# Setup in the order of tile 0, and products of constants in five waits of TensorE

## The chip, the cores and the metric

The kernel runs on one core of a Trainium2 chip. A core has TensorE (PE: matmuls and transposes, results in PSUM), VectorE (DVE), ScalarE (ACT), GpSimd (POOL) and SyncE (SP, which issues most DMAs). Each engine executes its own instructions in the order in which they are written; they wait for one another by semaphores. The metric is the device time of one launch in microseconds (us).

## The reference

Four transformer-like layers run in a row over `x` of 64 sequences x 64 tokens x 256 channels, all modulated by a condition vector per sequence:

```python
# L0: modulated layernorm, attention of 16 heads x 16, projection, second modulated layernorm
gamma = w @ Wg.T + bg;  beta = w @ Wb.T + bb
h   = gamma * (layernorm(x) * ln_g + ln_b) + beta
qkv = h @ Wqkv.T + bqkv
h1  = softmax(q k^T) / 16 @ v @ Wp.T + bp + x
x   = gamma * (layernorm(h1) * ln_g + ln_b) + beta + h1
# L1: attention of 16 heads x 64 with normalised q and k; then 8 experts, each takes its top 512 of 4096 tokens
shift = silu(t) @ W_ada.T + b_ada
h   = layernorm(x) * g + b + shift
...
tok = tok.at[idx].add(gate * (gelu(ln(tok[idx]) @ fc1 + b1) @ fc2 + b2))
# L2: modulated attention of 16 heads x 64, feed-forward 256 -> 1024 -> 256 with gelu
# L3: RMS norm, attention of 16 heads x 16 with rotary positions, gated feed-forward
```

Everything is float32.

## The kernel before, in words

The 4096 tokens stand as 32 tiles of 128 tokens (two sequences each) and 256 channels; `x` stays in SBUF. The program of each engine is written out by hand, layer by layer: setup, L0 (`pe_narrow`, `dve_narrow`, `act_narrow`, `pool_narrow`), L1 (`pe_attention`, ...), routing, the eight experts (`pe_ff` with `Q["moe"]`), L2, its feed-forward, L3, its feed-forward. No scheduler moves anything: the order on an engine is the order of the code, and `after`/`wait_ge` are the semaphore waits.

**Setup.** SP loads the constants, the columns and the condition (`ld["small"]`), then four tiles of `x` (`x0`), the modulation weights of L0 and L1 (`m0`, `m1`), the next four tiles (`x1`), the L0 weights (`ld["l0"]`, two loads) and the rest. DVE measures mean and variance of tiles 0 to 7 and takes their inverse roots by three Newton steps (`dve_first_block`, twelve small instructions; the thirteenth, `dve_shift`, gives `shift`), then prepares many constants for later layers (`dve_setup`), and last turns the modulation products that PE left in `psS` into the tables `g0`, `b0`, `g1`, `b1`. `su["table"]` tells that they are there; `following(eng, "setup")` is the wait for it. PE multiplies the condition by `m0` and `m1` (`pe_setup`), waits for the tables, and transposes `g0` and `b0` into rows, which ACT copies out (`rows0`, sent to DRAM for L1).

**Tile 0 of L0.** ACT normalises tile n (`normalise`: `x * rstd + shift`), PE transposes it (`turn_x`), ACT applies the tables (`modulate`), PE makes q and k (`qk`), ACT adds the bias (`biased`), PE makes v (`values`), ACT copies it; `bias_product` goes between. PE runs `turn_x(0)`, `qk(0)`, `turn_x(1)`, `values(0)`, `bias_product`, `qk(1)`, `turn_x(2)`, `values(1)`, and then the loop over tiles begins with `scores(0)`.

**The later places.** In L1 and L2 the last tile (31) has no next tile whose projections could fill PE's wait for the softmax. Before the first expert's products PE waits for the normalised tokens after `turn(0, 0)` and `turn(0, 1)`. Before L2, all outputs of the experts are added in DRAM (`moe_sum`), and the first tiles are loaded back before DVE can normalise them; PE's first instruction there is `pe_transpose_x(pe, L, 0)`.

In the trace one float32 matmul of the program is two records (x8 is four matmuls), and so is a load of weights.

Of the kernel before, what the change touches and what calls it, by code (L numbers as in the profile page):

```python
# [128 lines left out]
def build_program(nc, A, out):  # L129
    ctx = ExitStack()  # L130
    with ctx:
# [196 lines left out]

        def pe_transpose_x(pe, L, n):
# [149 lines left out]
        def pe_attention(pe, L):  # L479
# [6 lines left out]
            def first():  # L486
                pe_transpose_x(pe, L, 0)
# [7 lines left out]
            def step(t, ahead, behind):  # L495
# [12 lines left out]
                else:  # L508
                    finish_before()
                    if L.li == 2:  # L510
                        after(pe, L.s["v"], NT)
                        for k in range(KC):
                            pe_ff_turn(pe, Q["l2"], 0, k)
                pe_transpose_probs(pe, L, t)
# [153 lines left out]
        def pe_narrow(pe, L):  # L668
# [10 lines left out]
            else:  # L679
                pe.wait_ge(L.ready, 16 * L.loads)  # L680
                turn_x(0, 0)
                qk(0)
                turn_x(1, 0)
                values(0, 2)
# [3 lines left out]
                values(1, 3)  # L688
            pe.wait_ge(su["bias"], 1 if L.li == 0 else 2)
# [85 lines left out]
        def dve_first_block(v, ch):  # L775

            for i in range(2):
                v.wait_ge(ld[f"x{i}"], 16)
                dve_group_moments(ch, i)
            dve_rsqrt(ch, rstd[:, 0:8], moments[:, 0:8, 1])  # L780
            dve_shift(0, 8)
# [402 lines left out]
        def act_narrow(a, L):  # L1184
# [15 lines left out]
            def normalise(n):  # L1200

                a.wait_ge(su["shift"], max(1, n // 4))
# [22 lines left out]
            if L.li == 0:  # L1225
                normalise(0)
                normalise(1)
            modulate(0, 0)
# [3 lines left out]
            biased(0)  # L1232
            if L.li == 0:
# [325 lines left out]
        def pe_ff(pe, Q):  # L1559
# [732 lines left out]
        def pe_setup(pe):  # L2292

            pe.wait_ge(ld["small"], 48)
            pe.wait_ge(ld["first"], 16)
# [5 lines left out]
            pe.wait_ge(su["table"], 1)  # L2301
# [5 lines left out]
            pe.wait_ge(su["rows"], 1)  # L2307
# [30 lines left out]
        def act_setup(a):  # L2338
            a.wait_ge(ld["small"], 48)
            nc.scalar.activation(silT, condT, ACT.Silu).then_inc(su["silu"], 1)  # L2340
            a.wait_ge(su["turned_rows"], 1)
# [13 lines left out]

        def dve_setup(v, ch):
            v.wait_ge(ld["small"], 48)
            ch.reset()
# [4 lines left out]
            ch.link(nc.vector.tensor_scalar(c("l0_bv", 0, 2), c("l0_bv", 0, 2), 1.0 / 16, None, ALU.mult))  # L2363
            ch.link(nc.vector.tensor_copy(table("g1"), over_batches(c("l1_g", 0, 2))))
            ch.link(nc.vector.tensor_reduce(head_mask[:, 0:8], ident.rearrange("p (a s) -> p a s", s=16), AX.X, ALU.add))
# [543 lines left out]
```

## Time and profile before

| | before |
|---|---|
| device time, median of 3 runs | 2655.84 us (2652.8 to 2656.27) |
| the profiled execution's own time | 2656.11 us |
| its span, first to last instruction | 2654.3 us |
| PE busy | 2477.9 us, 93% of the span |
| DVE busy | 1775.8 us, 67% |
| ACT busy | 1208.9 us, 46% |
| POOL busy | 509.4 us, 19% |
| chain of work that ended last | PE 79%, DMA 7%, DVE 7%, issue 2%, ACT 2%, POOL 2% |
| mean granted TensorE clock | 0.971 |

Times in all rows are microseconds from the span's start unless marked ns. The granted clock is 1.00 at 2.4 GHz and 0.50 at 1.2 GHz. L572 is line 572 of the kernel before. A row's "idle before" in square brackets is how long its engine had sat idle, and what ended that. DVE busy 67% is an average: in the first 42 us PE waits for chains of small instructions, and later it is nearly always busy.

### The profile page before, as it was taken

What the parts mean: (1) busy time and instruction counts of PE and PEld (TensorE: products, weight loads), DVE (VectorE), ACT (ScalarE), POOL (GpSimd) and SP (SyncE); (2) the same over time, 40 slices, a digit from 0 to 9 for tenths busy, and PEclk for the clock granted to TensorE, in tenths of its full rate; (3) what the DMA queues carried; (4) which work ended last, traced back from release to release, by engine and by line L of the source; (5) the groups of instructions that cost most, each with busy time, mean ns of one, the idle gap of its engine ahead of it and who ended that gap; (6) DMA issues with size and microseconds to landing.
All of it is one profiled execution on the core that took longest, in us unless ns stands there. A gap on an engine that the chain in (4) does not pass through costs nothing.

```text
span 2654.3 us, 64384 instructions
## 1 busy us (share of the span) xinstructions
PE 2477.9 (93%) x25825; PEld 1938.8 (73%) x25825; DVE 1775.8 (67%) x3968; ACT 1208.9 (46%) x2524; POOL 509.4 (19%) x488
## 2 busy tenths in 40 slices
PE   6999699999999965999899999999999899989999
PEld 5887366666666644888788888887766677779998
DVE  4888688788887766554445545545555499877676
ACT  4887365556555621343233333333343577633333
POOL 1323010001000104554111011011001256600000
PEclk9999899999999966999899999999999999999999
DMA  6000000000000032453300000000000133300000
GB/s 219 3 3 2 20 25 24 24 32 24 24 24 32 16 105 62 132 142 64 130 0 0 0 0 0 0 0 1 1 1 0 34 115 112 103 9 9 17 17 17
DMA packets 72165, 102.28 MB, mean 39 GB/s; under 512 B 10880, under 2 KB 50304, under 8 KB 71488
## 3 DMA queue, kind: packets, MB, share of 16 engines
q1 hardware_dynamic: 65856, 91.46, 10.7%
q0 software_dynamic: 6144, 8.56, 1.7%
q8 instruction: 111, 1.82, 0.3%
q14 instruction: 54, 0.44, 0.1%
HBM read 67.20 MB, written 32.80 MB: 38 GB/s over the span
## 4 chain that ended last, share of the span: by engine, by line
PE 79%; DMA 7%; DVE 7%; issue 2%; ACT 2%; POOL 2%; SPq 1%; DVEq 0%; ACTq 0%; POOLq 0%
PE psW L349 17%; PE psW L342 9%; PE psP L1569 8%; DMA rotated<-work 6%; PE psP L461 4%; PE psS L1758 4%; PE psP L468 4%; PE psS L1768 4%; PE psO L1569 4%; PE psO L441 3%; PE psS L408 3%; PE psW L572 3%; PE psO L373 2%; PE psP L424 2%; PE psW L1569 2%
## 5 line engine op out<-in xcount | busy, mean ns | idle before, releaser
L349 PE MATMUL psW<-r,work 128*128 128x512 f32 x1024 | 481.7, 604 | 1.0 <-DVE work L866 1.0
L1393 POOL TENSOR_TENSOR work<-work 128x512 f32<-128x512 f32 x128 | 132.0, 1042 | 1133.7 <-DVE work L900 1133.6
L349 PEld LDWEIGHTS psW<-r,work 128*128 128x128 f32 x1024 | 180.7, 191 | 162.4 <-issue 156.8
L342 PE MATMUL psW<-work,r 128*128 128x128 f32 x2048 | 245.3, 279 | 1.3 <-DVE work L866 1.0
L342 PEld LDWEIGHTS psW<-work,r 128*128 128x128 f32 x2048 | 236.4, 194 | 4.2 <-DVE work L866 1.4
L1301 ACT ACTIVATE work<-work 128x512 f32<-128x512 f32 x128 | 80.1, 625 | 278.0 <-DVE work L879 278.0
L864 DVE TENSOR_TENSOR work<-psW,tab 128x256 f32<-128x256 f32 x64 | 27.0, 422 | 185.0 <-PE psW L335 185.0
L572 PE MATMUL psW<-work,r 128*128 128x128 f32 x1024 | 132.8, 283 | 8.0 <-ACT work L1194 5.7
L2106 ACT ACTIVATE work<-psP 128x512 f32<-128x512 f32 x64 | 38.2, 597 | 214.6 <-PE psP L1569 214.6
L572 PEld LDWEIGHTS psW<-work,r 128*128 128x128 f32 x1024 | 121.1, 194 | 16.0 <-ACT work L1194 6.6
L1569 PE MATMUL psP<-r 128*128 128x256 f32 x512 | 127.0, 386 | 5.0 <-DVE r L1845 3.0
L468 PEld LDWEIGHTS psP<-work,r 128*128 128x128 f32 x992 | 118.0, 192 | 14.8 <-issue 7.4
L461 PE MATMUL psP<-r,work 128*128 128x256 f32 x512 | 127.5, 383 | 1.2 <-ACT work L1317 1.2
L1174 ACT ACTIVATE work<-psO,col 128x512 f32<-128x512 f32 x128 | 92.5, 773 | 75.7 <-PE psO L373 75.6
L1317 ACT ACTIVATE work<-psO 128x512 f32<-128x512 f32 x128 | 69.5, 595 | 118.1 <-PE psO L441 118.1
L468 PE MATMUL psP<-work,r 128*128 128x128 f32 x992 | 120.7, 275 | 0.0
L1250 ACT ACTIVATE work<-work 128x512 f32<-128x512 f32 x128 | 80.6, 630 | 80.9 <-DVE work L890 78.6
L922 DVE RECIPROCAL work<-psO 128x256 f32<-128x256 f32 x64 | 112.1, 1751 | 0.9 <-PE psO L556 0.9
L1758 PE MATMUL psS<-work,r 128*128 128x512 f32 x256 | 111.5, 593 | 0.3 <-ACT work L2149 0.3
L1569 PEld LDWEIGHTS psP<-r 128*128 128x128 f32 x512 | 97.5, 193 | 19.4 <-DVE r L1845 3.4
L461 PEld LDWEIGHTS psP<-r,work 128*128 128x128 f32 x512 | 93.4, 192 | 24.9 <-ACT work L1317 8.8
L877 DVE TENSOR_REDUCE work<-psS 128x8 f32<-128x512 f32 x128 | 87.8, 686 | 33.5 <-PE psS L408 33.5
(353 smaller groups left out, 5495.8 us busy)
## 6 DMA issues: line engine op xcount, KB each, us to landing
r<-in_l_fc SPq DMA_DIRECT2D x16, 1024.0 KB
rotated<-work SPq DMA_DIRECT2D x60, 256.0 KB
work<-mod_rows SPq DMA_DIRECT2D x64, 128.0 KB, 2.9
work<-rotated SPq DMA_DIRECT2D x30, 256.0 KB
r<-in_l_w SPq DMA_DIRECT2D x2, 3072.0 KB, 14.6
x<-in_x SPq DMA_DIRECT2D x8, 512.0 KB, 9.3
gather_table<-work SPq DMA_DIRECT2D x32, 128.0 KB, 1.8
moe_sum<-work SPq DMA_DIRECT2D x32, 128.0 KB, 1.7
```

The costliest lines, as they stand in the source:

```text
L342: ins = nc.tensor.matmul(ps[:, q * P:(q + 1) * P], w[:, k, lo + q * P:lo + (q + 1) * P], L.hT[:, k, :], start=(k == 0), stop=(k == KC - 1))
L349: ins = nc.tensor.matmul(ps[:, 0:width], L.hT[:, k, :], w[:, k, lo:lo + width], start=(k == 0), stop=(k == KC - 1))
L461: ins = nc.tensor.matmul(psP[:, 0:D], L.oT[:, j, :], l1_wout[:, j, :], start=(j == 0), stop=(j == FJ - 1))
L468: ins = nc.tensor.matmul(out_bank(L, t)[:, q * P:(q + 1) * P], l2_wout[:, j, q * P:(q + 1) * P], L.oT[:, j, :], start=(j == 0), stop=(j == ...
L572: ins = nc.tensor.matmul(psW1[:, q * P:(q + 1) * P], w[:, k, q * P:(q + 1) * P], L.hT[n % L.far][:, k, :], start=(k == 0), stop=(k == KC - 1))
L877: ch.link(nc.vector.tensor_reduce(mx, ps, AX.X, ALU.max))
L922: ch.link(nc.vector.reciprocal(L.rec, psO[:, 256:512].rearrange("p (k n) -> p k n", n=P)))
L1174: nc.scalar.activation(L.qk[:, 4 * i:4 * i + 4, :], ps, ACT.Identity, bias=c("l1_qn", g + 1), scale=c("l1_qn", g)).then_inc(L.s[f"e{i}"].s ...
L1393: nc.gpsimd.tensor_tensor(E, E, halves(L.rs)[i].unsqueeze(2).broadcast_to([P, 8, N]), ALU.mult).then_inc(L.s[f"prob{i}"].sem, 1)
L1569: ins = nc.tensor.matmul(bank[:, 256 * i:256 * i + 256], w[:, at:at + P], h, start=first and i == 0, stop=i == 1, skip_group_check=True)
L1758: ins = nc.tensor.matmul(psS[:, q * 512:(q + 1) * 512], Q.w2[u][:, j, q * P:(q + 1) * P], Q.hid[:, j, :], start=(n == 0), stop=(n == FJ - 1))
L1768: ins = nc.tensor.matmul(ps, Q.hid[:, j, r * P:(r + 1) * P], Q.w2[u][:, j, :], start=(n == 0), stop=(n == FJ - 1))
```

## The change

Three things are changed.

1. **DVE's setup is in another order.** The first block of four tiles (moments, roots, shift) comes first, then the modulation tables `g0` and `b0` (and with them `su["table"]`), then the second block of four, and only then the constants and `b1`. There are now two root blocks of four columns where there was one of eight. `normalise(n)` waits for its own block.
2. **PE and ACT don't wait for the whole setup before tile 0.** `normalise(0)` and `turn_x(0)` no longer wait for the tables; the weights are waited for after `turn_x(0)`. The transposes of `g0` and `b0` and ACT's copy of them are now inside tile 0 (`pe_mod_rows`, `act_mod_rows`), behind `su["mask4"]`. The load of `l0_w` goes ahead of that of `x1`.
3. **`pe_keep_busy(bank, times)`** multiplies the identity by 256 columns of constants into a PSUM bank that nobody reads, in five places: 5 times while the first loads are under way, 5 in the last tile of L1, 4 before the first expert, 10 and 6 before L2 (the 6 behind a wait for the first rows loaded back), 6 in the last tile of L2.

```diff
+        def pe_keep_busy(bank, times):
+            for _ in range(times):
+                nc.tensor.matmul(bank[:, 0:256], ident, consts[:, 0:256], start=True, stop=True)
 # pe_attention, first():
+                if L.li == 2:
+                    pe_keep_busy(psS, 10)
+                    pe.wait_ge(ld["first"], 32)
+                    pe_keep_busy(psS, 6)
                 pe_transpose_x(pe, L, 0)
 # pe_attention, step(), last tile only:
+                    pe_keep_busy(psO, 6 if L.li == 2 else 5)
                 pe_transpose_probs(pe, L, t)
 # pe_narrow, L0:
+                turn_x(0, 0)
                 pe.wait_ge(L.ready, 16 * L.loads)
-                turn_x(0, 0)
                 qk(0)
                 turn_x(1, 0)
+                pe_mod_rows(pe)
                 values(0, 2)
 ...
                 values(1, 3)
+                pe.wait_ge(su["rows"], 1)
 # DVE
-        def dve_first_block(v, ch):
-            for i in range(2):
-                v.wait_ge(ld[f"x{i}"], 16)
-                dve_group_moments(ch, i)
-            dve_rsqrt(ch, rstd[:, 0:8], moments[:, 0:8, 1])
-            dve_shift(0, 8)
+        def dve_first_block(v, ch, i):
+            lo, hi = 4 * i, 4 * i + 4
+            v.wait_ge(ld[f"x{i}"], 16)
+            dve_group_moments(ch, i)
+            dve_rsqrt(ch, rstd[:, lo:hi], moments[:, lo:hi, 1])
+            dve_shift(lo, hi)
 ...
-            dve_first_block(v, ch)
+            dve_first_block(v, ch, 0)
+            dve_modulation(v, ch)
+            dve_first_block(v, ch, 1)
             dve_setup(v, ch)
 # act_narrow
-                a.wait_ge(su["shift"], max(1, n // 4))
+                a.wait_ge(su["shift"], n // 4 + 1)
 ...
                 normalise(1)
+                a.wait_ge(su["table"], 1)
             modulate(0, 0)
             modulate(1, 0)
             normalise(2)
             biased(0)
+                act_mod_rows(a)
 # pe_ff
                 turn(0, 1)
+                pe_keep_busy(psS, 4)
 # pe_setup
             pe.wait_ge(ld["small"], 48)
+            pe_keep_busy(psW0, 5)
             pe.wait_ge(ld["first"], 16)
 ...
-            pe.wait_ge(su["table"], 1)
+        def pe_mod_rows(pe):
+            pe.wait_ge(su["mask4"], 1)
             for i, name in enumerate(("g0", "b0")):
 ...
-            pe.wait_ge(su["rows"], 1)
 # SP
+            sp.dma_start(l0_w, chunked("l0_w")).then_inc(ld["l0"], 16)
             load_x(1)
-            sp.dma_start(l0_w, chunked("l0_w")).then_inc(ld["l0"], 16)
```

DVE at the start, before: the roots of eight tiles, then (rows left out here are constants) the tables last. `newton` is the scratch of the roots, `cond` and `tab` hold modulation and tables.

```order
L739 SCALAR_TENSOR_TENSOR rstd<-newton 128x8
L785 SCALAR_TENSOR_TENSOR shift<-moments,rstd 128x8
L63 ISA
L2363 TENSOR_SCALAR col<-col 128x2
L2364 COPY tab<-col 128x128
L2365 TENSOR_REDUCE head_mask<-consts 128x8
...
L2380 TENSOR_TENSOR head_mask<-head_mask 128x4
L2361 TENSOR_TENSOR cond<-psS,col 128x256
L2361 TENSOR_TENSOR tab<-cond,col 128x128
L2361 TENSOR_TENSOR cond<-cond,col 128x128
```

And now, from the end of the first root block on:

```order
L751 SCALAR_TENSOR_TENSOR rstd<-newton 128x4
L797 SCALAR_TENSOR_TENSOR shift<-moments,rstd 128x4
L2380 TENSOR_TENSOR cond<-psS,col 128x256
L2380 TENSOR_TENSOR tab<-cond,col 128x128
L2380 TENSOR_TENSOR cond<-cond,col 128x128
L2387 TENSOR_TENSOR tab<-cond 128x128
L763 BN_STATS stat<-x 128x6 x4
L766 BN_AGGR mv<-stat 128x2 x4
L768 COPY moments<-mv 128x8
```

The four table instructions stand behind the first shift; the second block and all constants moved behind them.

PE at the start, before. L2288 is the modulation, L2305 the transposes of the tables, L335 `turn_x`, L572 `qk`, L594 `values`:

```order
L2288 MATMUL psS<-cond,r 128x64 x12
L2305 MATMUL psS<-consts,tab 64x128 x4
L335 MATMUL psW<-consts,work 128x128 x2
L572 MATMUL psW<-work,r 128x128 x8
L335 MATMUL psW<-consts,work 128x128 x2
L594 MATMUL psW<-r,work 64x128 x8
```

And now (L332 are the products of constants, L2324 the transposes of the tables):

```order
L332 MATMUL psW<-consts 128x256 x5
L2304 MATMUL psS<-cond,r 128x64 x12
L340 MATMUL psW<-consts,work 128x128 x2
L582 MATMUL psW<-work,r 128x128 x8
L340 MATMUL psW<-consts,work 128x128 x2
L2324 MATMUL psS<-consts,tab 64x128 x4
L604 MATMUL psW<-r,work 64x128 x8
```

The transposes of the tables moved from ahead of `turn_x(0)` to behind `turn_x(1)`, and five products of constants stand ahead of everything.

PE from the last expert to L2's first q and k, before:

```order
L1768 MATMUL psS<-r,work 128x256 x16
L1768 MATMUL psP<-r,work 128x256 x16
L335 MATMUL psW<-consts,work 128x128 x2
L342 MATMUL psW<-work,r 128x128 x32
L349 MATMUL psW<-r,work 128x512 x4
```

And now:

```order
L1783 MATMUL psS<-r,work 128x256 x16
L1783 MATMUL psP<-r,work 128x256 x16
L332 MATMUL psS<-consts 128x256 x16
L340 MATMUL psW<-consts,work 128x128 x2
L347 MATMUL psW<-work,r 128x128 x32
```

Sixteen products now stand between the experts and the first transpose (L340), which waits for `xn`; the eleventh of them waits for `ld["first"]`.

## Rows read from the trace of the kernel before

**Rows 1.** Chain that ended last, 0 to 60 us: start, us, what

```profile
41.59 0.25 PE psP L607 x2
```

**Rows 2.** Timeline, 0 to 45 us: start, us, engine, line, idle before

```profile
7.58 1.41 DVE L751 BATCH_NORM_STATS2 stat<-x 128x6 f32<-128x256 f32 x4 [7.58 <-DMA x<-in_x]
...
9.10 5.35 PE L2288 MATMUL psS<-cond,r 128*128 128x64 f32 x24 [9.10 <-DMA r<-in_l_mod]
...
11.26 1.41 DVE L751 BATCH_NORM_STATS2 stat<-x 128x6 f32<-128x256 f32 x4 [1.66 <-DMA x<-in_x]
...
13.32 0.17 DVE L733 TENSOR_SCALAR newton<-moments 128x8 f32<-128x8 f32 x1
...
15.76 0.17 DVE L785 SCALAR_TENSOR_TENSOR shift<-moments,rstd 128x8 f32<-128x8 f32 x1
...
19.64 0.42 DVE L2361 TENSOR_TENSOR cond<-psS,col 128x256 f32<-128x256 f32 x1
...
21.75 1.06 PE L2305 MATMUL psS<-consts,tab 128*64 128x128 f32 x4 [7.29 <-DVE tab L2389]
22.85 0.59 ACT L2342 ACTIVATE work<-psS 64x512 f32<-64x512 f32 x1 [17.99 <-PE psS L2305]
...
25.34 1.27 ACT L1194 ACTIVATE work<-psW,tab 128x64 f32<-128x64 f32 x4
```

**Rows 3.** DMA issues, 0 to 50 us: KB each, us to landing

```profile
r<-in_l_w SPq DMA_DIRECT2D x1, 768.0 KB, 8.2
...
r<-in_l_wp SPq DMA_DIRECT2D x1, 256.0 KB, 8.4
```

**Rows 4.** Windows of L572: stretch, its us, PE busy, PEld busy, PEclk, DMA, GB/s

```profile
26.00:30.50 4.50, 3.79 (x16) 3.49 (x16) 1.00 1.04 403
42.00:44.30 2.30, 2.05 (x16) 1.86 (x16) 1.00 0.08 9
```

**Rows 5.** Windows: PE, PEld, DVE, ACT, POOL busy, then PEclk

```profile
944.00:954.00 10.00, 6.50 (x78) 5.54 (x79) 2.10 (x6) 2.28 (x4) 2.01 (x2) 0.50 0.01 2
...
1033.00:1043.00 10.00, 6.53 (x17) 4.99 (x17) 6.73 (x9) 1.19 (x2) 7.83 (x6) 0.50 0.21 56
```

**Rows 6.** Timeline at the end of L1, last tile

```profile
942.72 0.61 PE L476 MATMUL psP<-r,work 128*128 128x8 f32 x4 [2.06 <-ACT work L1287]
...
946.29 1.97 PE L424 MATMUL psP<-consts,work 128*128 128x128 f32 x8 [2.96 <-DVE gates L1032]
...
951.39 5.11 PE L461 MATMUL psP<-r,work 128*128 128x256 f32 x16 [1.21 <-ACT work L1317]
```

**Rows 7.** Timeline at the first expert

```profile
1031.88 1.97 PE L1555 MATMUL psW<-consts,work 128*128 128x128 f32 x8
...
1037.31 3.78 PE L1569 MATMUL psP<-work,r 128*128 128x256 f32 x8 [3.47 <-DVE work L1845]
...
1046.24 1.89 PE L1569 MATMUL psP<-work,x 128*128 128x256 f32 x8
```

**Rows 8.** Timeline at the start of L2

```profile
1266.74 0.75 DVE L761 BATCH_NORM_STATS2 stat<-x 128x6 f32<-128x256 f32 x2 [6.78 <-DMA x<-moe_sum]
...
1270.75 0.66 PE L335 MATMUL psW<-consts,work 128*128 128x128 f32 x2 [11.64 <-DVE work L850]
...
1272.38 10.31 PE L342 MATMUL psW<-work,r 128*128 128x128 f32 x64 [0.98 <-DVE work L866]
```

**Rows 9.** Timeline of L2, tile 1: the same 64 records

```profile
1288.34 7.41 PE L342 MATMUL psW<-work,r 128*128 128x128 f32 x64
```

**Rows 10.** Timeline at the end of L2, tiles 30 and 31

```profile
1843.25 3.73 PE L468 MATMUL psP<-work,r 128*128 128x128 f32 x32
...
1848.28 1.04 PE L1555 MATMUL psW<-consts,work 128*128 128x128 f32 x8
...
1852.94 2.02 PE L424 MATMUL psP<-consts,work 128*128 128x128 f32 x8 [3.63 <-POOL work L1393]
...
1858.09 5.77 PE L468 MATMUL psS<-work,r 128*128 128x128 f32 x32 [1.21 <-ACT work L1317]
```

More of the change, by code:

```diff
@@ L1232, in act_narrow @@
             biased(0)
+            if L.li == 0:
+                act_mod_rows(a)
             if L.li == 0:
@@ L2340, in act_setup, with act_mod_rows @@
             nc.scalar.activation(silT, condT, ACT.Silu).then_inc(su["silu"], 1)
+        def act_mod_rows(a):
             a.wait_ge(su["turned_rows"], 1)
@@ L2354, in by_batch, with dve_modulation, tt @@
             return ps[:, lo * B:(lo + n) * B].rearrange("p (k b) -> p k b", b=B)
+        def dve_modulation(v, ch):
+            def tt(out, a, b, op=ALU.add):
+                ch.link(nc.vector.tensor_tensor(out, a, b, op))
+            v.wait_ge(ld["small"], 48)
+            v.wait_ge(su["mm"], 1)
+            tt(mod[:, 0:4, :], by_batch(psS, 0, 4), over_batches(c("l0_bgb", 0, 4)))
+            tt(table("g0"), mod[:, 0:2, :], over_batches(c("l0_g", 0, 2)), ALU.mult)
+            tt(mod[:, 4:6, :], mod[:, 0:2, :], over_batches(c("l0_b", 0, 2)), ALU.mult)
+            nc.vector.tensor_tensor(table("b0"), mod[:, 4:6, :], mod[:, 2:4, :], ALU.add).then_inc(su["table"], 1)
         def dve_setup(v, ch):
-            v.wait_ge(ld["small"], 48)
-            ch.reset()
             def tt(out, a, b, op=ALU.add):
@@ L2363, in dve_setup @@
             ch.link(nc.vector.tensor_scalar(c("l0_bv", 0, 2), c("l0_bv", 0, 2), 1.0 / 16, None, ALU.mult))
+            ch.link(nc.vector.tensor_reduce(head_mask[:, 0:8], ident.rearrange("p (a s) -> p a s", s=16), AX.X, ALU.add))
+            tt(mod[:, 6:8, :], by_batch(psS, 4, 2), over_batches(c("l1_bada", 0, 2)))
+            nc.vector.tensor_tensor(head_mask[:, 8:12], head_mask[:, 0:4], head_mask[:, 4:8], ALU.add
+                                    ).then_inc(su["mask4"], 1)
+            tt(table("b1"), mod[:, 6:8, :], over_batches(c("l1_b", 0, 2)))
             ch.link(nc.vector.tensor_copy(table("g1"), over_batches(c("l1_g", 0, 2))))
-            ch.link(nc.vector.tensor_reduce(head_mask[:, 0:8], ident.rearrange("p (a s) -> p a s", s=16), AX.X, ALU.add))
             ch.link(nc.vector.tensor_reduce(slot_rows[:, 0, 0:E8], ident.rearrange("p (t e) -> p e t", e=E8), AX.X, ALU.add))
@@ L2379, in dve_setup @@
                                               ident.rearrange("p (a s e) -> p a s e", s=2, e=8)[:, :, 1 - s, :]))
-            nc.vector.tensor_tensor(head_mask[:, 8:12], head_mask[:, 0:4], head_mask[:, 4:8], ALU.add
-                                    ).then_inc(su["mask4"], 1)
-            v.wait_ge(su["mm"], 1)
-            tt(mod[:, 0:4, :], by_batch(psS, 0, 4), over_batches(c("l0_bgb", 0, 4)))
-            tt(table("g0"), mod[:, 0:2, :], over_batches(c("l0_g", 0, 2)), ALU.mult)
-            tt(mod[:, 4:6, :], mod[:, 0:2, :], over_batches(c("l0_b", 0, 2)), ALU.mult)
-            tt(table("b0"), mod[:, 4:6, :], mod[:, 2:4, :])
-            tt(mod[:, 0:2, :], by_batch(psS, 4, 2), over_batches(c("l1_bada", 0, 2)))
-            nc.vector.tensor_tensor(table("b1"), mod[:, 0:2, :], over_batches(c("l1_b", 0, 2)), ALU.add
-                                    ).then_inc(su["table"], 1)
         def dve_setup2(v, ch, i):
@@ L2771, in _ @@
             pe_setup(pe)
-            following(pe, "setup")
             pe_narrow(pe, L[0])
@@ L2807, in _ @@
             act_setup(a)
-            following(a, "setup")
             act_narrow(a, L[0])
```

## The prediction

> **What bounds the kernel now.** I read the table of busy times first. TensorE (PE) is busy 93% of the span and makes 79% of the chain that ended last, so only two things can be gained: stretches where PE waits, and stretches where it works at half its clock. Then the chain of the first 60 us. The reader is to see that the loop over tiles begins only at 41.59 us, with the scores of tile 0 [rows 1]; what stands ahead of it is paid in full. The timeline of that stretch shows how it is paid: x lands at 7.58 and the modulation products run from 9.10 to 14.45, but the tables are there only at 21.75, since VectorE (DVE) first takes the roots of eight tiles and fills constants of later layers, and ScalarE (ACT) can modulate tile 0 only at 25.34 [rows 2].
>
> Last the clock. The same sixteen records of L572 take 3.79 us at 26 us and 2.05 us at 42 us [rows 4]: the ratio, 1.85, is that of 1.2 to 2.4 GHz with a little overhead. The granted clock stands at 1.00 in both rows; in the first stretch there is no record of it yet, so I go by the pace. Later the record and the pace agree: 0.50 from 944 to 954 and from 1033 to 1043 [rows 5]. Each half-clock stretch follows one in which PE mostly waited: 2.06 and 2.96 us in the last tile of L1 [rows 6], 3.47 us before the first expert after a thin routing stage [rows 7], 11.64 us before L2 [rows 8], 3.63 us in the last tile of L2 [rows 10]. Each is on PE's path, and behind the last three PE is nearly always busy, so what they cost is carried to the end.
>
> **The change part by part: setup.** DVE's moments of four tiles take from 11.26 to 13.32, 2.06 us; the first block now ends at 7.58 + 2.06 = 9.64. Twelve root instructions and the shift take from 13.32 to 15.93, 2.6 us, at 0.17 us each on eight columns; I take the same for four, so the second root block adds 2.6 us to DVE, but behind the tables. The first shift is at 12.25. The modulation products are ready at 14.45, four table instructions take 1.4 us (of the six from 19.64 to 21.75): tables at 15.9 in place of 21.75. PE transposes tile 0 at 14.5 (0.7 us), ACT normalises tile 1 behind it (0.6 us), and modulates tile 0 at 15.95 in place of 25.34: 9.4 us earlier. Only 5.8 of that is DVE's order. The other 3.6 is that PE's transposes of the tables (1.06), ACT's copy (0.59), the normalisation and the transposes of tile 0 no longer stand between tables and modulation.
>
> From there to the scores it was 41.59 - 25.34 = 16.25 us. Three things change in it. ACT's copy and PE's transposes of the tables now lie inside: 0.6 and 0.5 to 1.1 us. The transposes wait for mask4, which DVE gives after the second block (2.06 + 2.6) and four short instructions (1.0): at 21.6; PE's second transpose_x would be done at 15.95 + 1.3 + 3.8 + 0.7 = 21.75, so nothing waits if q and k run at half clock. Against it PE works without a break from 17.2 on, so the full clock, which showed by 36 us before, should come by 24: the products of v and the bias (about 4 us at half clock) save 1.9. Together 9.4 + 1.1 = 10.5 us, the low bound.
>
> Five products of constants run from about 4.6. The nearest rows of that shape are the experts': 3.78 us for eight records, four products, at half clock and 1.89 at full [rows 7], so 0.95 or 0.47 us each. At half clock they end at 9.35, 0.25 us after m0 landed. If they bring the full clock at once, the modulation takes 3.0 in place of 5.35 us (24 records at the 0.123 us of the fast row of L572 [rows 4]), tables come at 13.8, modulation of tile 0 starts at 14.0, q and k end at 17.3; but then PE waits 2 us for mask4 (19.6). By the same steps the scores start at 28.0: 13.6 us, the high bound. I take the middle, 12.
>
> The loads: l0_w (768 KB) now goes ahead of x1. It landed 8.2 us after its issue and l0_wp 8.4 after its own [rows 3], by about 14, before q and k ask for them (15.3 at the earliest). x1 landed at 11.26; 768 KB more ahead of it at the 403 GB/s of [rows 4] is 1.9 us, 13.2, and it is now wanted at 13.8 to 15.9. Both are covered; a landing 3 us later would show as a later mask4. The constants that DVE moves back (3.7 us, 15.93 to 19.64) end by about 25 and are hidden behind PE's first products: DVE is next wanted for tile 0's softmax.
>
> **The four later places.** All are in-order queues: what waits behind the products is PE's next real product, and behind it ACT or DVE.
>
> End of L1: PE is free at 943.33 and goes on at 946.29 [rows 6]; five products take 2.35 us at full clock (hidden) or 4.75 at half (1.8 late). If the full clock holds, the transposes save 0.9 of 1.97 and the sixteen records of L461 take two times 1.89 in place of 5.11, 1.3; with the small products between them at most 2.6. But 2.06 us of waiting ahead of them stay. I take 1.4.
>
> First expert: four products from 1033.85 take 3.8 us at half clock, to 1037.65, 0.3 late at most. PE then has no pause from 1031.9 on, and the full clock, which came at 1043 [rows 5], should be there at or soon after 1037.3 [rows 7]: half of the 5.7 us between is 2.85. I take 2.5; low bound -0.3.
>
> Start of L2: PE is free from 1259.1. Ten products end at 1263.8, six follow the first rows (at the earliest seen, 1266.74) and end at 1269.6, before the transposes at 1270.75 [rows 8]. At full clock the first 64 records take 7.41 in place of 10.31 us [rows 9]: 2.9, high bound with the transposes 3.2. At half clock the six end at 1272.4 if the ten ended in time and at 1274.3 if they ran on: 3.6 late, low bound. Between the three bursts PE still waits 2.9 and 1.1 us; copies by DVE between the blocks take some of the gain. I take 1.7.
>
> End of L2: free at 1849.32, wanted at 1852.94 [rows 10]; six products take 2.8 us at full clock, hidden, or 5.7 at half, 2.1 late. Gain: 5.77 - 3.73 = 2.0 for L468, and about 0.7 on the transposes and small products. I take 2.7.
>
> Sum: 12 + 1.4 + 2.5 + 1.7 + 2.7 = 20.3 us. The profiled execution took 2656.11 (span 2654.3), so 2635.8; it lies 0.27 above the median of the runs, 2655.84, so 2635.5.
>
> The moment at which the clock returns is not tied to the work: it took 5.7 us of dense work at the first expert and about 6.3 in L2 by the pace of [rows 8]. The Trainium skill, "TensorE: Matmul & The Clock Gate", part 1 on the clock gate, says that this varies from run to run, the same kernel showing 6, 11 or 14 slow matmuls at its start. No row of one execution can show that; by that rule the 20.3 us would be 17 to 24 with the run.
>
> **The rivals.** (a) The products of constants are hidden but don't hold or bring the clock, since waits of 1 to 3 us stay beside them. For it: PE fell to half clock at L1's end though no wait there was over 3 us. Then only the setup's low bound is left, 10.5, less about 0.5 of lateness: 2646. (b) The setup's start is given back: tiles 0 to 4 are then held by DVE, which also measures two further tiles for each of them, or by loads not yet landed (DMA's share is 1.04 at 26 to 30 us [rows 4]). For it: DVE is at 67% and more in L0; against it: nothing in the first tiles waits for a load before, and a tile's chain is the same wherever it starts. Setup worth 4, the rest 8.3: 2643.5. (c) Slower: PE is at half clock when it reaches the products, and all run late: 1.8 + 0.3 + 3.6 + 2.1 = 7.8 us behind which real work stands. This decides only when the setup gives less than that; with nothing from the setup 2663.6. Against it: 5.8 us of the setup's gain are DVE's order alone.
>
> **How the numbers follow.** Forecast 0.75, with a range of its own from 2629 to 2641; (a) 0.12; (b) 0.11; (c) 0.02. Time 2635.5. The range goes from 2628 (every place at its high bound: 13.6 + 2.6 + 2.85 + 3.2 + 3, less what phases take) to 2645, which takes in (b) and part of (a). About 0.2% (5.3 us) is what a measurement can tell from no change. Faster by more: 0.96; within: 0.02; slower: 0.02.
>
> **What would show it.** In the profile after, DVE's first table instruction at 14.5 or earlier, ACT's first modulation at 14 to 16, the first scores at 28 to 31. If they stand there and the time is not 10 us shorter, (b) holds. The transposes of the last tile of L2 at 1.1 us for eight records and its L468 at 3.7 (in L1: sixteen records of L461 at 3.8); L2's first 64 records near 7.4; the first expert's eight records at 1.9. If these stay at 2.0, 5.1, 10.3 and 3.8, (a) holds. If a real product starts later than the end of the wait that it had before, (c) has a part. I am wrong if the time is over 2645 or under 2628.

## The result and the profile after

| | before | after |
|---|---|---|
| median of the runs | 2655.84 us (2650.46 to 2657.99, 5 runs) | 2639.05 us (2637.57 to 2643.38, 5 runs) |
| the profiled execution's own time | 2656.11 us | 2642.82 us |
| its span | 2654.3 us | 2641.0 us |
| mean granted TensorE clock | 0.971 | 0.975 |

The ratio of after to before is 0.9945, with a 95% interval from 0.9931 to 0.9959: 14.6 us faster, between 10.9 and 18.3 (the two medians lie 16.8 us apart). The forecast of 2635.5 us was 3.6 us low and its range held the time. A second series of after gave 2642.65 us (2635.61 to 2646.67, 6 runs) and 0.9948. The profiled execution of after lies 3.8 us above the first median, so its sums are made against the profile of before, 13.3 us.

First the setup, in the timeline of after (start, us, engine, line, idle before). It answers to [rows 1, 2].

```profile
9.15 2.89 PE L2304 MATMUL psS<-cond,r 128*128 128x64 f32 x24 [0.34 <-DMA r<-in_l_mod]
...
9.85 0.17 DVE L745 TENSOR_SCALAR newton<-moments 128x4 f32<-128x4 f32 x1
...
12.34 0.42 DVE L2380 TENSOR_TENSOR cond<-psS,col 128x256 f32<-128x256 f32 x1
...
14.15 1.27 ACT L1206 ACTIVATE work<-psW,tab 128x64 f32<-128x64 f32 x4
...
15.56 3.52 PE L582 MATMUL psW<-work,r 128*128 128x128 f32 x16 [2.03 <-ACT work L1206]
...
19.25 0.63 PE L2324 MATMUL psS<-consts,tab 128*64 128x128 f32 x4
...
28.16 0.32 PE L617 MATMUL psP<-work 32*64 32x128 f32 x2
```

DVE's roots stand on four columns and begin at 9.85; its first table instruction follows at 12.34, the first modulation at 14.15 in place of 25.34, and the first scores at 28.16 in place of 41.59: 13.4 us. The modulation products ran at full clock (2.89 us for 24), and then q and k of tile 0 fell back to half (3.52 us for 16), after 2.03 us of waiting. The transposes of the tables (L2324) waited for nothing.

Some 2 us of the 13.4 belong not to the change but to the one execution of before that was profiled. There the products of v of tile 0 went at half pace, in before:

```profile
32.26 1.97 PE L594 MATMUL psW<-r,work 128*64 128x128 f32 x16 [1.38 <-ACT work L1194]
```

One experiment below, the four later groups alone, has before's setup unchanged. In its profile the same products, in nearly the same place, went at full pace:

```profile
31.96 1.09 PE L604 MATMUL psW<-r,work 128*64 128x128 f32 x16 [1.38 <-ACT work L1204]
```

The bias products behind them took 1.13 us in place of 2.05, and its first scores stand 2.1 us ahead of before's. So two executions of one setup differ by that much.

What comes next wasn't in the forecast: windows of after across L0's end and L1's start (busy us of PE, PEld, DVE, ACT, POOL, then the granted clock, the share of the DMA engines and GB/s).

```profile
250.00:254.00 4.00, 2.82 (x43) 2.10 (x43) 2.50 (x6) 0.60 (x1) 1.04 (x1) 0.60 0.02 4
254.00:282.00 28.00, 9.13 (x16) 4.07 (x16) 15.44 (x51) 1.23 (x2) 0.00 (x0) 0.57 0.05 19
...
292.00:302.00 10.00, 8.76 (x84) 6.21 (x85) 5.78 (x12) 3.74 (x5) 0.00 (x0) 0.50 0.01 2
```

And the timeline of PE there, in after:

```profile
251.27 1.08 PE L639 MATMUL psO<-work,pair_sums 128*32 128x256 f32 x8 [1.18 <-DVE work L935]
...
257.59 1.99 PE L566 MATMUL psO<-r,work 128*128 128x256 f32 x4 [2.79 <-DVE x L941]
274.68 0.66 PE L340 MATMUL psW<-consts,work 128*128 128x128 f32 x2 [15.10 <-DVE work L862]
...
292.18 4.02 PE L378 MATMUL psO<-consts,work 128*128 128x128 f32 x16 [1.53 <-DVE work L1010]
297.15 1.98 PE L413 MATMUL psS<-work 64*64 64x64 f32 x64 [0.96 <-ACT work L1186]
```

At L0's end the granted clock was 0.50 between 250.8 and 254.2, amid waits of 1.08, 0.66 and 1.18 us, and 0.50 again from 257.6 on, behind the wait of 2.79. Before fell in L0's last tiles too, at another point (0.52 from 258.0 to 261.5).

And in before, the same instructions of L1's tile 0:

```profile
302.95 1.26 PE L373 MATMUL psO<-consts,work 128*128 128x128 f32 x8 [1.53 <-DVE work L998]
304.56 1.30 PE L373 MATMUL psO<-consts,work 128*128 128x128 f32 x8 [0.36 <-ACT work L1174]
306.82 1.16 PE L408 MATMUL psS<-work 64*64 64x64 f32 x64 [0.96 <-ACT work L1174]
```

The waits are those of before, but the clock is 0.50 where before had full pace, so sixteen records take 4.02 us in place of 2.91 with their pause, and the 64 small ones 1.98 in place of 1.16. The change touches no instruction there.

The end of L1, timeline of after. It answers to [rows 6].

```profile
935.07 0.61 PE L481 MATMUL psP<-r,work 128*128 128x8 f32 x4 [2.06 <-ACT work L1302]
935.54 3.29 PE L332 MATMUL psO<-consts 128*128 128x256 f32 x10
938.64 1.89 PE L429 MATMUL psP<-consts,work 128*128 128x128 f32 x8
...
943.20 3.72 PE L466 MATMUL psP<-r,work 128*128 128x256 f32 x16 [1.20 <-ACT work L1332]
```

The ten records of constants (L332) fill the wait of 2.96 us. The transposes still go near half pace (1.89), the last sixteen records at full (3.72 in place of 5.11): y is ready at 946.92 in place of 956.50, 9.6 us ahead, where L1's last tile stood 7.6 ahead: 2.0 us won.

The first expert, timeline of after. It answers to [rows 7].

```profile
1020.32 1.76 DVE L1819 TENSOR_SCALAR work<-work 128x256 f32<-128x256 f32 x4 [6.81 <-DMA work<-gather_table,slots]
...
1024.65 2.39 PE L332 MATMUL psS<-consts 128*128 128x256 f32 x8
...
1028.33 1.99 PE L1584 MATMUL psP<-work,r 128*128 128x256 f32 x8 [1.29 <-DVE work L1861]
...
1032.13 5.36 DVE L1819 TENSOR_SCALAR work<-work 128x256 f32<-128x256 f32 x4
...
1037.42 1.26 POOL L1543 TENSOR_TENSOR x<-r,x 128x512 f32<-128x512 f32 x1
1037.53 1.18 DVE L1828 COPY work<-work 128x4 f32<-128x4 f32 x1
...
1038.77 0.66 PE L1570 MATMUL psW<-consts,work 128*128 128x128 f32 x4 [1.53 <-DVE work L1828]
```

The first records stand 9.0 us ahead of before, the second products 9.8: 0.8 us won. The full clock is there (1.99 us for eight records in place of 3.78). But PE then waits 1.53 us for DVE's normalisation of the next tokens and a copy of four columns behind it, which takes 1.18 us and ends just as GpSimd's product (L1543) does.

The start of L2, timeline of after. It answers to [rows 8].

```profile
1250.20 4.58 PE L332 MATMUL psS<-consts 128*128 128x256 f32 x20 [0.91 <-DVE work L1993]
...
1257.01 4.54 PE L332 MATMUL psS<-consts 128*128 128x256 f32 x12 [2.22 <-DMA x<-moe_sum]
1261.39 0.38 PE L340 MATMUL psW<-consts,work 128*128 128x128 f32 x2
...
1262.74 5.62 PE L347 MATMUL psW<-work,r 128*128 128x128 f32 x48 [0.98 <-DVE work L878]
...
1269.01 2.05 PE L347 MATMUL psW<-work,r 128*128 128x128 f32 x16 [0.64 <-DVE work L1032]
```

The second burst ran at half clock and ended after DVE's normalisation (1260.43 and 0.41 us), so the transposes come some 0.4 us late; the 64 records then take 8.3 us with a wait for DVE's copy, in place of 10.31.

The end of L2, timeline of after. It answers to [rows 10].

```profile
1837.49 2.75 PE L332 MATMUL psO<-consts 128*128 128x256 f32 x12
1841.28 0.63 PE L429 MATMUL psP<-consts,work 128*128 128x128 f32 x4 [1.03 <-POOL work L1408]
...
1845.51 3.84 PE L473 MATMUL psS<-work,r 128*128 128x128 f32 x32 [1.19 <-ACT work L1332]
```

Here all went as forecast: full clock through the wait, 3.84 us in place of 5.77.

The ledger. Each number is by how many us the instruction starts earlier in the named profile than in that of before (whose start is in the first column), read from PE's timeline. One profile per kernel: differences of one or two microseconds between columns prove nothing.

| start of | before | after | after again | no constants | no setup constants | L1 start | more constants | no expert |
|---|---|---|---|---|---|---|---|---|
| L0's scores, tile 0 | 41.5 | 13.4 | 12.2 | 11.1 | 11.5 | 10.7 | 14.5 | 13.1 |
| L0's scores, tile 31 | 257.5 | 13.2 | 12.1 | 11.1 | 11.5 | 10.1 | 14.3 | 12.5 |
| L1's first transposes | 285.7 | 11.0 | 9.8 | 10.2 | 9.3 | 8.0 | 14.3 | 12.5 |
| L1's scores, tile 1 | 326.4 | 7.4 | 6.2 | 10.3 | 8.1 | 10.5 | 15.2 | 13.4 |
| L1's scores, tile 31 | 939.1 | 7.6 | 6.3 | 10.4 | 8.3 | 10.5 | 15.5 | 13.6 |
| first expert's second products | 1053.2 | 9.8 | 8.2 | 9.5 | 11.1 | 13.1 | 17.9 | 16.2 |
| L2's scores, tile 1 | 1305.1 | 11.6 | 9.8 | 10.0 | 13.0 | 14.9 | 19.8 | 18.0 |
| L2's scores, tile 31 | 1846.9 | 11.7 | 9.8 | 10.0 | 13.0 | 14.9 | 19.8 | 18.0 |
| L3's scores, tile 0 | 2104.3 | 14.5 | 12.7 | 10.2 | 15.9 | 17.8 | 22.5 | 19.3 |
| the end | 2649.3 | 13.3 | 13.4 | 11.6 | 16.3 | 16.8 | 19.3 | 19.9 |

After wins 13.4 us in the setup, loses 6.0 between L0's last tile and L1's second, and wins 2.2 to the first expert, 1.8 to L2, 2.8 at L2's end; 1.2 go in L3.

The same reading of the other five profiles:

| start of | later groups alone | order of PE, ACT, SP | order of DVE | five of the setup alone | doubled |
|---|---|---|---|---|---|
| L0's scores, tile 0 | 2.1 | 3.3 | 2.5 | 12.0 | 11.2 |
| L0's scores, tile 31 | 2.0 | 3.3 | 2.4 | 11.4 | 11.1 |
| L1's first transposes | -0.8 | 1.4 | 2.4 | 9.1 | 8.9 |
| L1's scores, tile 1 | -0.7 | -0.2 | 2.6 | 7.9 | 5.2 |
| L3's scores, tile 0 | 6.4 | -0.3 | 5.7 | 11.7 | 8.5 |
| the end | 6.2 | -4.4 | 7.3 | 9.6 | 9.1 |

Two stretches show how much one execution decides. From L0's first scores to L1's tile 1, after, after again and doubled lose 6.0 us each and the five alone 4.1, all with the products in the setup; the profiles without them lose from nothing (order of DVE, and before by definition) to 3.5 (order of PE, ACT, SP). From L1's tile 1 to L3, the profiles with all four later groups at their counts win 6.5 to 7.8 us; but those with none of them win -0.1 twice, 3.1 and 3.8. Before's profile is among the slowest of its kind there, so a win measured against it is larger than what the products are worth. In L3, where no kernel has products, the profiles range from 1.6 won to 4.1 lost.

### The profile page after: what moved, and what is told of

The parts are those of the page before. It is cut to its first block, busy times and chain, and to the rows that moved or that the text cites. A ratio compares the mean times of both kernels' runs of the same rounds, so it can differ in the third digit from the quotient of the medians.

```text
span 2641.0 us, 64540 instructions
## 1 busy us (share of the span) xinstructions
PE 2486.5 (94%) x25897; PEld 1943.6 (74%) x25897; DVE 1778.7 (67%) x3981; ACT 1209.8 (46%) x2524; POOL 510.0 (19%) x488
## 4 chain that ended last, share of the span: by engine, by line
PE 81%; DVE 7%; DMA 5%; issue 2%; ACT 2%; POOL 2%; SPq 1%; DVEq 0%; ACTq 0%; POOLq 0%
PE psW L354 17%; PE psW L347 8%; PE psP L1584 8%; PE psP L466 4%; DMA rotated<-work 4%; PE psS L1773 4%; PE psP L473 4%; PE psS L1783 4%; PE psO L1584 4%; PE psW L582 4%; PE psS L413 3%; PE psO L446 3%; PE psO L378 3%; PE psP L429 2%; PE psW L1584 2%
## 5 line engine op out<-in xcount | busy, mean ns | idle before, releaser
L1584 PEld LDWEIGHTS psP<-r 128*128 128x128 f32 x512 | 96.9, 192 | 19.3 <-DVE r L1861 3.4
```

The lines of the kernel that those rows point to most:

```text
L1584: ins = nc.tensor.matmul(bank[:, 256 * i:256 * i + 256], w[:, at:at + P], h, start=first and i == 0, stop=i == 1, skip_group_check=True)
```

## The experiments

Each was run beside before in the same series; ratios are to before, with the 95% interval. The shared edit is the count of constant products; "after" or "before" says which kernel it starts from.

### No constants (from after)

```diff
 def pe_keep_busy(bank, times):
-    for _ in range(times):
+    for _ in range(0):
         nc.tensor.matmul(bank[:, 0:256], ident, consts[:, 0:256], start=True, stop=True)
```

> The changed kernel with every product of constants left out: only the new order of the setup. My theory: the order alone gives what the first scores gained, less what PE's clock gave: they start at 30 to 31 us (28.16 in the changed kernel, 41.52 before), and the stages in the last tile of L1 and L2, at the first expert and at L2's start are at half clock again as before. Time about 2645 us, 10 to 11 below the kernel before. Rival 1 (the products do nothing for the time): 2639, as the changed kernel. Rival 2 (the order gives little and the products most): 2650 or more.

Measured: 2643.82 us (2639.78 to 2649.17, 6 runs), 0.9962 [0.9949, 0.9976]. One row of its setup, q and k at half pace:

```profile
17.40 3.75 PE L582 MATMUL psW<-work,r 128*128 128x128 f32 x16 [2.56 <-ACT work L1206]
```

And its windows at L0's end and in L1's tile 0:

```profile
250.00:254.00 4.00, 1.89 (x26) 1.32 (x30) 3.86 (x8) 1.92 (x4) 0.00 (x0) 1.00 0.00 0
...
292.00:302.00 10.00, 7.99 (x90) 4.74 (x91) 7.46 (x14) 5.67 (x10) 0.58 (x1) 1.00 0.01 2
```

The order alone brings the first scores 11.1 us ahead (the low bound said 10.5) and the end 11.6 in the profile; the runs say 10.1 us (6.4 to 13.5), as forecast. This profile kept the full clock where after lost it, and 10.3 us of its lead reach L1.

### The four later groups alone (from before)

```diff
+def pe_keep_busy(bank, times): ...
 def first():
+    if L.li == 2:
+        pe_keep_busy(psS, 10)
+        pe.wait_ge(ld["first"], 32)
+        pe_keep_busy(psS, 6)
...
+                    pe_keep_busy(psO, 6 if L.li == 2 else 5)
...
                 turn(0, 1)
+                pe_keep_busy(psS, 4)
```

> The kernel before with only the four later groups of products (5 in L1's last tile, 4 at the first expert, 16 at L2's start, 6 in L2's last tile), the setup as it was. My theory: the places keep what the changed kernel's profile showed, 2.0 + 0.8 + 1.8 + 2.8 us, so about 2649 us; L2's last tile is at full clock (eight records of its transposes 1.1 us, 32 of L468 in 3.8). Rival 1 (the products do nothing for the time): 2656. Rival (products run late): over 2656.

Measured: 2650.08 us (2646.6 to 2652.64, 11 runs), 0.9984 [0.9976, 0.9993], which is 4.2 us (1.9 to 6.4). That fits the 2649 expected here and the 4.5 us by which after's ratio and that of no constants differ, and is half of the 8.3 that the prediction had for the four places. Its profile wins 7.1 us over them and ends 6.2 us ahead; the table above says why the profile shows more than the runs.

### PE's, ACT's and SP's order alone (from before)

```diff
     turn_x(0, 0)
+    pe.wait_ge(L.ready, 16 * L.loads)
     qk(0)
     turn_x(1, 0)
+    pe_mod_rows(pe)
...
     normalise(1)
+    a.wait_ge(su["table"], 1)
 modulate(0, 0)
...
+    act_mod_rows(a)
...
-load_x(1)
 sp.dma_start(l0_w, chunked("l0_w")).then_inc(ld["l0"], 16)
+load_x(1)
```

> The kernel before with only the order of PE, ACT and SP changed (normalisation and transposes of tile 0 ahead of the tables, rows copied inside tile 0); VectorE's setup stays as it was and there are no products of constants. My theory: the tables stand at 21.7 us as before and tile 0 is modulated right behind them, at 21.8 in place of 25.34: first scores near 38, time 3 to 4 us below the kernel before, 2652. Rival (the gain of the setup is all VectorE's order): 2656, first scores at 41.5.

Measured: 2653.51 us (2647.96 to 2660.68, 12 runs), 1.0 [0.9988, 1.0012]. Two rows of its setup:

```profile
13.33 1.41 DVE L753 BATCH_NORM_STATS2 stat<-x 128x6 f32<-128x256 f32 x4 [3.53 <-DMA x<-in_x]
...
23.79 1.29 ACT L1196 ACTIVATE work<-psW,tab 128x64 f32<-128x64 f32 x4 [3.72 <-DVE tab L2398]
```

The tables come at 23.75, not at the 21.7 of before that was expected. The moved load is the reason: x1 lands behind l0_w, at 13.3 in place of 11.26 (the prediction had 13.2), and DVE in its old order takes the roots of all eight tiles only then. In after nothing waits for x1. So this half alone pays 2.1 us for the load, the first scores are only 3.3 us ahead, and the time doesn't show it.

It also shows the loss at L1's start without a single product of constants and with before's instructions in L1:

```profile
302.00:309.00 7.00, 5.73 (x75) 4.05 (x76) 3.46 (x7) 2.90 (x5) 0.00 (x0) 0.54 0.01 2
```

The granted clock is 0.54 from 302 to 309 us, and of its lead of 3.3 us nothing is left at L1's tile 1.

### DVE's order alone (from before)

```diff
-def dve_first_block(v, ch):
+def dve_first_block(v, ch, i):
...
+def dve_modulation(v, ch): ...
...
-            pe.wait_ge(su["table"], 1)
+            pe.wait_ge(su["mask4"], 1)
```

PE's transposes of the tables stay ahead of tile 0, and now wait for mask4. SP's load order is the new one here too.

> Only VectorE's new order of the setup (and the load of l0_w ahead of x1); PE and ACT wait for the whole of it as in the kernel before: the tables' transposes, now behind mask4, stand ahead of tile 0, and there are no products of constants. My theory: the two halves of the new order need each other. mask4 comes at 21.6 us, where the tables came before (21.7), so the transposes start at the same time, first scores at 41 to 41.5, time as before, 2653 to 2656. Rival (VectorE's order alone earns 5.8 us): first scores at 35.7, 2649.

Measured: 2653.12 us (2648.78 to 2661.82, 12 runs), 0.9996 [0.9983, 1.001]. One row of PE's timeline:

```profile
21.10 1.06 PE L2320 MATMUL psS<-consts,tab 128*64 128x128 f32 x4 [7.02 <-DVE head_mask L2393]
```

The tables are early and nobody can use them: PE's queue holds tile 0 behind transposes that wait 7.02 us. First scores 2.5 us ahead (at 39.0, where 41 to 41.5 was expected), which is no more than the 2.1 of the profile whose setup is before's. The halves give nothing measurable in the time, 0.0 us (-3.2 to 3.2) and 1.1 (-2.7 to 4.5); together they give 10.1 (6.4 to 13.5).

### The five of the setup alone (from after)

```diff
-            pe_keep_busy(psW0, 5)
+            for _ in range(5):
+                nc.tensor.matmul(psW0[:, 0:256], ident, consts[:, 0:256], start=True, stop=True)
```

with pe_keep_busy empty.

> The changed kernel with only the first five products of constants, those ahead of the modulation; none in L1, at the expert, in L2. My theory: they bring the full clock for the modulation in some runs, 2 us earlier first scores (28.2 to 30.9), and all later places are at half clock; time 2641.5, between the new order alone (2643.8) and the changed kernel (2639.05). Rival (the five earn nothing, since the clock falls again while PE waits for tile 0): 2643.8.

Measured: 2643.46 us (2639.1 to 2646.49, 6 runs), 0.9949 [0.9931, 0.9967]. Against no constants the medians differ by 0.4 us and the ratios by 0.0013, less than either interval. That is the rival's time (2643.8), not the 2641.5 of the theory, though the first scores stand 12.0 us ahead: 4.1 of them are gone at L1's tile 1.

### All counts doubled (from after)

```diff
-            for _ in range(times):
+            for _ in range(2 * times):
```

> The changed kernel with twice as many products in each of the five places (10; 10; 8; 20 and 12; 12). My theory: the products are free only while they end inside the wait. At 0.43 us each (full clock) the doubled ones run over by 2 us in the setup, 1.5 in L1's last tile, 1.7 at the expert, 3 at L2's start and 1.3 in L2's last tile: 9 to 10 us, time 2648.5. Rival (they keep the clock better, and PE has slack): 2639 or less.

Measured: 2645.94 us (2642.47 to 2647.33, 7 runs), 0.996 [0.9945, 0.9975]. Its timeline:

```profile
4.57 7.58 PE L332 MATMUL psW<-consts 128*128 128x256 f32 x20 [4.57 <-DMA cond<-in_condT]
...
11.99 2.79 PE L2304 MATMUL psS<-cond,r 128*128 128x64 f32 x24
...
1252.63 14.08 PE L332 MATMUL psS<-consts 128*128 128x256 f32 x64 [0.91 <-DVE work L1993]
```

Once a group is longer than its wait, real products stand behind it: the modulation starts 2.8 us later than in after. By the medians 6.9 us are lost, by the ratios 4.0 (their intervals overlap) and by the profiles 4.2; 9 to 10 were expected. No count between one and two times after's was run.

### 28 products at L1's start (from after)

```diff
 def first():
+    if L.li == 1:
+        pe_keep_busy(psS, 24)
...
     if L.li == 1:
+        pe_keep_busy(psS, 4)
         pe_l1_turn(pe, L, 0, range(4))
```

> The changed kernel with two more groups of products: 24 while PE waits 15 us between L0 and L1, and 4 ahead of the transposes of L1's first q and k. In the changed kernel's profile PE ran at half clock from L0's last tile into L1's second, and of the 13.2 us won by then 5.8 were gone at L1's second scores. My theory: that loss is the clock alone; with the products the L1 start is at full clock and about 3.6 of the 5.8 us are kept (2.2 fall in L0's last tiles, ahead of them): lead at L1's second scores 11 us, time 2635.5. Rival 1 (the loss is waits for loads or VectorE, which stay): lead 7.4 us, 2639. Rival 2 (24 products at half clock run past the wait, 20 us in place of 10): 5 us later, 2644.

Measured: 2638.29 us (2636.81 to 2640.59, 5 runs), 0.9942 [0.9929, 0.9954]. Its timeline at L1's start:

```profile
292.45 1.21 PE L378 MATMUL psO<-consts,work 128*128 128x128 f32 x8
```

The first eight transposes of probabilities take 1.21 us with no pause ahead of them, and the lead from L1's first transposes to tile 1 grows by 2.5 us where after's shrinks by 3.6. Here the setup happened to win only 10.7, so the profile ends well ahead and the median just 0.8 us below after's: the ratios don't differ. The lead at L1's tile 1 is 10.5, where 11 was expected, so the clock and not the waits took the 3.6 us there; the time of 2635.5 wasn't reached.

### More constants (from the last)

```diff
-        pe_keep_busy(psS, 24)
+        pe_keep_busy(psS, 28)
...
+    pe_keep_busy(psP, 1)
     turn_x(0, 0)
     pe.wait_ge(L.ready, 16 * L.loads)
+    pe_keep_busy(psP, 4)
     qk(0)
     turn_x(1, 0)
+    pe_keep_busy(psP, 1)
...
     if not rotary:
+        pe_keep_busy(psS, 2)
     outputs(31)
...
+        pe_keep_busy(psS, 4)
```

The last two groups stand in L0's end, ahead of its last outputs and last projection.

> The changed kernel with products also in the waits that it leaves: 1, 4 and 1 around tile 0's transposes in the setup, 2 and 4 in L0's last tile, 28 between L0 and L1, 4 ahead of L1's first transposed q. My theory: the clock no longer falls in the setup (q and k of tile 0 at full clock, 2.0 in place of 3.5 us, but mask4 then holds PE, so at most 0.5 us), in L0's last tiles (1 to 2 us) nor at L1's start (3 us): 2634.5. Rival 1 (DVE's small instructions and row loads bound these places, not the clock): 2639. Rival 2 (run over): over 2641.

Measured: 2634.92 us (2632.75 to 2636.79, 6 runs), 0.9919 [0.9902, 0.9937]. Its windows across L0's end and L1's start:

```profile
250.00:254.00 4.00, 3.82 (x52) 3.03 (x52) 3.02 (x6) 0.00 (x0) 1.04 (x1) 1.00 0.01 4
254.00:282.00 28.00, 23.17 (x81) 15.48 (x81) 16.32 (x57) 4.04 (x7) 0.00 (x0) 0.94 0.06 19
...
292.00:302.00 10.00, 10.00 (x83) 5.19 (x73) 8.54 (x19) 6.71 (x12) 2.09 (x2) 1.00 0.00 1
```

In the setup q and k of tile 0 now stand at full pace, and the next row waits for mask4, as the high bound had it:

```profile
15.29 2.02 PE L585 MATMUL psW<-work,r 128*128 128x128 f32 x16 [0.30 <-ACT work L1215]
...
18.97 0.63 PE L2333 MATMUL psS<-consts,tab 128*64 128x128 f32 x4 [1.00 <-DVE head_mask L2406]
```

The clock stays at or near 1.00 and the whole lead of 14.3 us reaches L1. The time is that of the theory (2634.5). All its runs lie below all of the first series of after, but one run of after's second series (2635.61) lies among them, and the intervals of the ratios touch; the version without the expert's four, below, settles it beside after in one series.

### After again

The same kernel a second time.

> The changed kernel itself once more, to see which of its profile's losses come back. Theory A (they belong to the program): of the lead that the first scores have (13.4 us in its first profile) some 4 to 6 us are gone again by the second tile of L1, since PE falls to half clock between L0 and L1, and DVE holds the first expert back by 1.5 us; time 2639 +- 1.5. Theory B (they belong to one execution): the lead at L1's second tile is 10 us or more here, and the time is the same within 1.5 us, since the median never held the loss.

Measured: 2642.65 us (2635.61 to 2646.67, 6 runs), 0.9948 [0.9934, 0.9962]. Theory A held in its profile: 12.1 us of lead at L0's tile 31, 6.2 at L1's tile 1, and PE again waits 1.53 us for the copy at the first expert. Its time was 2.2 us above what A allowed, while the ratio all but repeats the first series' 0.9945: the whole series lay higher, before too (2656.86).

### No setup constants (from after)

```diff
-            pe_keep_busy(psW0, 5)
```

> The changed kernel without the five products of the setup; the four later groups stay. Theory A: the five are worth what the first scores gain by them (2.3 us at most), carried to the end: 2641. Theory B: what they gain is given back between L0 and L1, since the versions with them lost 3.6 to 6 us there and the version without any products 0.8: first scores at 30.4, lead 11 us at the end of L0 and still 10 at L1's second tile, and a time equal to the changed kernel's or 1 to 3 us below it.

Measured: 2640.33 us (2638.47 to 2643.04, 5 runs), 0.9946 [0.9933, 0.9958], beside 0.9948 of after in the same series. The five bring nothing that can be measured. By the time B holds (equal to after's, or 1 to 3 us below: it is 2.3 below that of the same series). B's reason falls all the same in this profile: without them the lead also shrank, from 11.5 to 8.1 us. What they win by the profiles, 0.7 to 1.9 us at the first scores, is lost in the spread or at L1's start.

### More constants without those ahead of the first expert

```diff
                 turn(0, 1)
-                pe_keep_busy(psS, 4)
```

> The version with more constants, without the four ahead of the first expert; all else stays. What the four are worth is read from the lead gained between L1's last tile and the first expert's result, and from the time. Theory A (the full clock comes 5.7 us earlier and the work follows it, as forecast): 2.5 us, 2637.4. Theory B (DVE's normalisation of the next tokens holds the expert back, so that most of it turns into a wait): 1 us or less, 2635 to 2636, with PE waiting 1 us or less for DVE at the first expert's second group of records.

Measured: 2633.4 us (2632.11 to 2636.94, 5 runs), 0.992 [0.9907, 0.9933]. Its timeline at the first expert:

```profile
1021.46 3.78 PE L1593 MATMUL psP<-work,r 128*128 128x256 f32 x8 [3.48 <-DVE work L1869]
...
1027.44 4.49 DVE L1827 TENSOR_SCALAR work<-work 128x256 f32<-128x256 f32 x4
...
1030.50 1.27 POOL L1552 TENSOR_TENSOR x<-r,x 128x512 f32<-128x512 f32 x1
1031.96 0.17 DVE L1836 COPY work<-work 128x4 f32<-128x4 f32 x1
...
1032.67 0.60 PE L1579 MATMUL psW<-consts,work 128*128 128x128 f32 x4
```

The records are back at half clock (3.78), yet PE reaches the next tokens' transposes 11.2 us after its first record, where after reached them 10.4 us after (1038.77 less 1028.33). GpSimd's chain ends 10.3 us after the first record in both (1031.77 and 1038.68), and DVE's part is done behind it. So the four products are worth 0.8 us here, and nothing in the time: 2633.4 lies below what either theory said. Theory B's reason holds, that other engines bound the stage. The same series has after at 0.9948 [0.9934, 0.9962]; this version's interval ends just below that one, so the added products at the setup, L0's end and L1's start do beat after, by 7.4 us in the ratios.

## Why the prediction was right, and where its steps failed

**Setup: right in its steps, 13.4 against 12** (range 10.5 to 13.6), with some luck in the size. The order alone gave 11.1, near the low bound, and both halves of it are needed: early tables help only if PE and ACT have nothing in their queues ahead of tile 0. But the 1.9 us for the products of v and the bias at full clock were counted as the change's. They came in a profile with before's setup too (2.1 us at the first scores), so about 2 of the 13.4 us are the luck of before's one profile. The clock part was smaller than the high bound because q and k fell to half clock; with six more products they didn't (14.5). No row there waits for the reordered loads.

**What was missed: the way from L0 to L1.** The step that failed is that the setup's gain is carried to the end. I had looked at the clock only where before was slow, and took it that elsewhere the clock would stay as it was. But that before passed L1's first tile at full pace is no property of its program: with all instructions there unchanged, both profiles of after lost 6.0 us, and the order of PE, ACT and SP alone, with no products, lost 3.5. No constants and no setup constants are the same program up to L1's end, and lost 0.8 and 3.4. Products in these two places took the loss away in both profiles that had them, and the granted clock was 1.00 there in more constants where it was 0.60 and 0.50 in after: the clock is the cause. Since two executions of one program differ by 2.6 us, some of the loss goes with the execution. Whether the five products of the setup add to it isn't settled: the four profiles with them and no products at L1's start lost 4.1 to 6.0 us, those without them at most 3.5, but no run shows a way from one to the other.

**The end of L1: 2.0 against 1.4; the start of L2: 1.8 against 1.7; the end of L2: 2.8 against 2.7.** Right against before's profile, with the copy by DVE between the blocks taking its share, as said. But the forecast took before's half clock at these places as its rule, and it is not: two profiles with no later products won 3.1 and 3.8 us over before between L1's tile 1 and L3 all the same. Only the second burst at L2's start had a part of rival (c), 0.4 us late.

**First expert: mis-sized, 0.8 against 2.5.** The full clock came, even earlier than taken; the gain became a wait, since GpSimd's chain and DVE's normalisation behind it are late next. I had named who waits for PE, and not who PE waits for next.

**The rivals.** (a) is what no constants is: 2643.8 measured, 2646 forecast. It isn't what after does: the later places went to full clock. But in the time the later groups are worth 4.2 us, half of the 8.3, and the order alone came closer to after's time than the forecast had it. (b) had the right sign (part of the start is given back) at the wrong place: L0's 32 tiles together lost 0.2. (c) has a part for doubled counts; in after it is the 0.4 us at L2's start.

**The sum.** 20.3 forecast; in the profile 13.4 + 2.2 + 1.8 + 2.8 = 20.2 was won at the places named, 6.0 was lost again at L1's start and 1.2 in L3, and 0.3 came in small shifts: 13.3. Against that one profile the four places and the setup were sized right as a whole, and the 7 us came off elsewhere. Against before's runs they were too large (4.2 for 8.3), and the luck is that before's own profile had a late clock in the setup and a good one at L1's start. That the median is only 3.6 us above the forecast is because the profiled execution lies 3.8 above the median: the time came out closer than the working, by luck. The working's remark on the spread held: the first scores of after came 13.4 and 12.2 us ahead in two profiles of one kernel.

In the setup, q and k fell to half clock after 2.03 us of waiting with thin work about it; at L0's end the clock fell amid waits of at most 1.18 us, and again behind 2.79. The Trainium skill, "TensorE: Matmul & The Clock Gate", under why this matters for your kernels, says to leave no long pause between bursts of TensorE; the trace agrees where a pause was filled (1.00 through L2's end, where before waited 3.63 us and fell to half clock), and adds that several short ones in a row were not safe either.

## What to carry to other kernels

Read the granted clock also at places that are now fast: where PE waits a few microseconds with thin work about it, it can fall to half clock in one execution and not in the next, and a shift won upstream is lost there. Products of constants in such waits are worth it while they end before the wait does and nothing else is late next; one longer than its wait costs time. A gain read against a single profile holds that profile's luck: profile the kernel before more than once. When an order is changed over several queues, expect nothing from any half: the early result is used only when no queue holds its reader behind something later.

## What the runs showed that I had not expected

A copy of four columns by DVE took 1.18 us beside a GpSimd product of 128x512 and 0.17 us when it began after the last one; four normalisations of 128x256 took 5.36 and 4.49 us beside them and 1.76 at 1020.32, when GpSimd computed nothing. The Trainium skill, "SBUF — State Buffer", on who interferes with whom, says that the two engines can hold a shared pair of ports in turn, the second one blocked until the first has finished. The rows agree: the copy ends at 1038.71, GpSimd's product at 1038.68.

Before itself had medians of 2653.26, 2654.77 and 2656.86 us in the three later series, with single runs from 2646.86 to 2664.26. That this spread is in part the clock's is argued from the ledger, not shown.
